# Deformable convolution on one core: a quad's three sampling rounds joined into one visit to the row tiles

## The reference

```python
offset = _offset_conv(x, w_off)            # 3x3, 18 channels: dy, dx of nine taps
py = base_y.astype(x.dtype)[None] + dy
px = base_x.astype(x.dtype)[None] + dx
sampled = _bilinear_gather(x, py, px)      # nine bilinear samples per pixel
return jnp.einsum('bckhw,ock->bohw', sampled, w_conv.reshape(O, C, K * K))
...
x = x + _L0_conv_ref(_ln_c(x), L0_conv_w_off, L0_conv_w_conv)
```

## Time and profile before

| | us |
|---|---|
| median of 3 runs | 3994.7 |
| lowest and highest | 3988.97, 3998.19 |
| span of the profiled execution, first to last instruction | 3990.2 |
| TensorE busy in that span | 3781.9 (95%) |
| VectorE, ScalarE, GpSimd busy | 2579.8, 1794.4, 1553.5 |
| phase A in that span | about 0 to 2100 |

### The profile page before, as it was taken

How to read it: one execution, slowest core, us unless ns; L and a number is a source line. 1 busy time by engine, 2 the same in 40 slices (tenths; PEclk the granted TensorE clock), 3 DMA queues, 4 the chain that set the end, 5 groups by cost and what they waited for, 6 DMA issues and landing times. The chain is left out here.

```text
span 3990.2 us, 88376 instructions
## 1 busy us (share of the span) xinstructions
PE 3781.9 (95%) x31447; PEld 2461.4 (62%) x31447; DVE 2579.8 (65%) x8511; ACT 1794.4 (45%) x4685; POOL 1553.5 (39%) x2661
## 2 busy tenths in 40 slices
PE   6999999999999999999997999999999999997468
PEld 5666666666666666666663566666666666664245
DVE  4444444444444444444426999999999999996633
ACT  4555555555555555555530334344343434344124
POOL 4544545455444544445422333232323233333210
PEclk8999999999999999999997999999999999998755
DMA  6555555555555554555525777777777777885779
GB/s 117 102 97 96 91 93 95 89 101 93 88 97 91 101 92 89 95 91 91 88 47 194 270 276 268 276 269 277 266 278 271 275 271 270 280 300 175 270 292 394
DMA packets 611673, 709.79 MB, mean 178 GB/s; under 512 B 62256, under 2 KB 494256, under 8 KB 594848
## 3 DMA queue, kind: packets, MB, share of 16 engines
q1 hardware_dynamic: 505760, 630.17, 57.1%
q10 hardware_dynamic: 104448, 71.85, 5.8%
q0 software_dynamic: 1024, 2.10, 0.1%
HBM read 521.20 MB, written 181.63 MB: 176 GB/s over the span
## 5 line engine op out<-in xcount | busy, mean ns | idle before, releaser
L366 PE MATMUL a_ob<-a_sr,wcv 128*128 128x512 f32 (+3 forms) x2820 | 1081.6, 518 | 0.8 <-DVE a_xo L496 0.8
L436 ACT COPY a_sr<-a_sb 128x576 f32<-128x576 f32 (+7 forms) x1296 | 621.2, 562 | 903.9 <-PE a_sb L351 895.9
L351 PEld LDWEIGHTS a_sb<-a_tt,a_win 32*128 32x128 f32 x19008 | 655.7, 185 | 264.6 <-issue 247.7
L351 PE MATMUL a_sb<-a_tt,a_win 32*128 32x144 f32 x19008 | 748.6, 300 | 19.2 <-ACT a_sr L436 12.7
L521 POOL TENSOR_TENSOR a_sx<-a_hh 128x576 f32<-128x576 f32 x260 | 377.8, 1453 | 929.9 <-DVE a_hh L473 921.8
L366 PEld LDWEIGHTS a_ob<-a_sr,wcv 128*128 128x128 f32 x2820 | 491.3, 191 | 279.0 <-issue 231.5
L1116 DVE TENSOR_TENSOR b_P<-b_P,b_x 128x1024 f32<-128x1024 f32 x512 | 620.2, 1212 | 1.8 <-DMA b_P<-pd 1.8
L473 DVE TENSOR_SCALAR a_hh<-a_hh 128x576 f32<-128x576 f32 (+1 forms) x128 | 59.5, 465 | 841.0 <-ACT a_hh L415 841.0
L1019 PE MATMUL b_z<-b_P,b_ew 128*128 128x512 f32 x1024 | 463.4, 595 | 0.0
L1022 PE MATMUL b_z<-b_P,b_ew 128*128 128x512 f32 x1024 | 460.3, 592 | 0.0
L1245 POOL TENSOR_TENSOR b_ss<-b_st 128x12 f32<-128x12 f32 (+2 forms) x139 | 30.0, 216 | 1058.1 <-DVE b_pp L1190 963.8
(11 more groups left out here) (186 smaller groups left out, 5302.4 us busy)
## 6 DMA issues: line engine op xcount, KB each, us to landing
b_P<-pd SPq DMA_DIRECT2D x128, 2048.0 KB, 7.6
a_win<-xtp SPq DMA_DIRECT2D x2144, 36.0 KB
a_xin<-in_x SPq DMA_DIRECT2D x128, 256.0 KB, 6.3
xtp<-a_tn ACTq DMA_DIRECT2D x128, 256.0 KB, 2.3
x1d<-a_xo SPq DMA_DIRECT2D x128, 256.0 KB, 5.9
b_x<-x1d SPq DMA_DIRECT2D x128, 256.0 KB, 7.5
x2d<-b_xa SPq DMA_DIRECT2D x128, 256.0 KB, 3.4
pw<-x3d SPq DMA_DIRECT2D x128, 256.0 KB, 6.6
```

The costliest lines, as they stand in the source:

```text
L351: t = e.matmul(d[:, 0:3 * m_, :, NU_ * i:NU_ * i + NU_], win[32 * q:32 * q + 32, half_of(Q, j) % NWH, NWIN // 3 * h + i, :], m, start=(j = ...
L366: t = e.matmul(ob[:, r:r + m, :], k["wcv"][:, 3 * (2 - kr) + kx, :], rows[:, :, t_, :], start=(t_ == 0 and r == 0), stop=(t_ == 8))
L436: a = e.copy(bass.AP(d.tensor, d.offset, [list(d.ap[0]), [1152, ni], [1536, nk], [32, 4], [1, m]]), bass.AP(v.tensor, v.offset, [list(v.ap ...
```

## The change

A quad's three rounds stand together at slot 0 of the step (the small quad's at slot 12). Rounds 0 and 2 write to banks 0 to 3, round 1 to banks 4 to 7. These four are shared with the results of turn (bank 4), conv (5 and 6), shift (6) and out (7). So round 1 waits until the readers of all four are through (normed, mv_ready, y_ready, on_ready, x1_ready), and every full-array matmul waits until round 1's copy is through (bank_free). The second conv of a step, in the shift's bank, waits for on_ready, the offs of the same step. The copy out of the banks is a stage of its own, "evict", at slots 1, 2 and 3: ScalarE copies the quarters 0 and 1, VectorE 2 and 3, and each raises its own semaphore. Round 1's copy is done with two instructions of 432 columns on each engine, the others with three. The full-array work follows from slot 4 on: shift, turn, then out with the two convs between its taps.

```diff
@@ order_a
-        for h in range(3 if len(cs) else 0):
-            samples[t0 + 4 * h] = (quad_of(cs[0]), h)
-            if len(cs) > 4:
-                samples[t0 + 12 + 2 * h] = (quad_of(cs[4]), h)
+        if len(cs):
+            samples[t0] = quad_of(cs[0])
+        if len(cs) > 4:
+            samples[t0 + 12] = quad_of(cs[4])
...
+        if 0 <= Z < NG:
+            put(t0 + 4, "shift", Z)
+            put(t0 + 4, "offs", Z)
         if 0 <= F < NG:
-            put(t0 - 3, "turn", F)
-            put(t0 - 1, "stats", F)
-            put(t0 + 1, "scale", F)
-            put(t0 + 4, "conv", F, 0)
-            put(t0 + 8, "conv", F, 1)
-            put(t0 + 4, "norm", F, 0)
-            put(t0 + 5, "norm", F, 1)
-            put(t0 + 6, "norm_out", F)
-            put(t0 + 6, "y_out", F, 0)
-            put(t0 + 10, "y_out", F, 1)
+            put(t0 + 4, "turn", F)
+            put(t0 + 4, "stats", F)
+            put(t0 + 6, "scale", F)
+            put(t0 + 5, "conv", F, 0)
+            put(t0 + 6, "conv", F, 1)
+            put(t0 + 7, "norm", F, 0)
+            put(t0 + 7, "norm", F, 1)
+            put(t0 + 8, "norm_out", F)
+            put(t0 + 8, "y_out", F, 0)
+            put(t0 + 9, "y_out", F, 1)
         if 0 <= Z < NG:
-            put(t0 - 1, "zsum", Z)
-            put(t0 + 1, "shift", Z)
-            put(t0 + 2, "offs", Z)
-            put(t0 + 3, "offs_out", Z)
-            put(t0 + 4, "reach", Z)
-            put(t0 + 3, "place", Z)
-            put(t0 + 4, "hats", Z)
-            put(t0 + 7, "bend", Z)
-            put(t0 + 9, "clip", Z)
+            put(t0 + 1, "zsum", Z)
+            put(t0 + 5, "offs_out", Z)
+            put(t0 + 5, "place", Z)
+            put(t0 + 5, "hats", Z)
+            put(t0 + 6, "bend", Z)
+            put(t0 + 7, "reach", Z)
+            put(t0 + 7, "clip", Z)
         if 0 <= s - 2 < NG:
-            for t, slot in enumerate((1, 2, 3, 5, 6, 7, 9, 10, 11)):
+            for t, slot in enumerate((4, 5, 6, 7, 8, 9, 10, 11, 11)):
...
-            out.append(("sample", Q, h))
+            out.append(("sample", Q))
+        for h in range(3):
+            if slot - 1 - h in samples:
+                out.append(("evict", samples[slot - 1 - h], h))
@@ phase_a
-    TK = P("a_tk", [128, 4, 128])
-    YO = P("a_yo", [128, 512])
-    YB = [P("a_yb0", [128, 2, 162]), YO[:, 0:324].rearrange("p (r f) -> p r f", r=2)]
-    OF = YO[:, 324:396].rearrange("p (r f) -> p r f", r=4)
-    SB = P("a_sb", [128, 4, 512])
-    OB = P("a_ob", [128, 512])
+    SB = P("a_sb", [128, 8, 512])
+    TK = SB[:, 4, :].rearrange("p (r f) -> p r f", r=4)
+    YB = [SB[:, i, 0:324].rearrange("p (r f) -> p r f", r=2) for i in (5, 6)]
+    OF = SB[:, 6, 324:396].rearrange("p (r f) -> p r f", r=4)
+    OB = SB[:, 7, :]
...
+    def strips(Q, h, q0):
+        n, m_ = quad(Q)
+        b, c = centre(n)
+        R = b * H + c - 1
+        v = SB[:, 4 * (h % 2) + q0, 0:1]
+        if h == 1 and m_ == 4 and c >= 0:
+            for q in (0, 1):
+                d = sr[:, (R - 2) % NSR * 1152 + 12 * h + 32 * (q0 + q):][:, 0:1]
+                yield (bass.AP(d.tensor, d.offset, [list(d.ap[0]), [1152, 4], [1536, 3], [127, 3], [1, 12]]),
+                       bass.AP(v.tensor, v.offset + 512 * q, [list(v.ap[0]), [108, 4], [36, 3], [12, 3], [1, 12]]))
+            return
...
+        for kx in range(3):
+            x = max(0, 12 * h - kx)
+            m = min(31, 12 * h + 11 - kx) + 1 - x
+            for i, ni, kr, nk in parts:
+                d = sr[:, ((R - 2) % NSR + i + kr) * 1152 + kr * 384 + kx * 128 + x + 32 * q0:][:, 0:1]
+                yield (bass.AP(d.tensor, d.offset, [list(d.ap[0]), [1152, ni], [1536, nk], [32, 2], [1, m]]),
+                       bass.AP(v.tensor, v.offset + (9 * i + 3 * kr + kx) * 12 + x + kx - 12 * h,
+                               [list(v.ap[0]), [108, ni], [36, nk], [512, 2], [1, m]]))
@@ tensor
+        def bank_free():
+            w.wait_ge(taken_act, taken)
+            w.wait_ge(taken_dve, taken)
...
             elif o[0] == "conv":
                 _, G, h = o
+                bank_free()
                 w.wait_ge(y_ready, 4 * (G - 1) + 2 * h + 2)
                 if h:
-                    w.wait_ge(on_ready, min(G - 2, NG - 1) + 1)
+                    w.wait_ge(on_ready, shifts)
...
-                w.wait_ge(sr_ready, 3 * Q + h)
-                for i in range(NWIN // 3):
+                for h in range(3):
+                    if h == 1:
+                        w.wait_ge(normed, convs)
+                        w.wait_ge(mv_ready, convs // 2)
+                        w.wait_ge(y_ready, 2 * convs)
+                        w.wait_ge(on_ready, shifts)
+                        w.wait_ge(x1_ready, outs)
+                    else:
+                        w.wait_ge(taken_act, 3 * Q + h // 2)
+                        w.wait_ge(taken_dve, 3 * Q + h // 2)
+                    for i in range(NWIN // 3):
...
+                                d = SB[:, 4 * (h % 2) + q, 0:432].rearrange("p (k t x) -> p k t x", k=12, t=3)
...
+                    t.then_inc(sampled, 1)
+                taken = 3 * Q + 2
@@ scalar
-            elif o[0] == "sample":
+            elif o[0] == "evict":
...
+                for d, v in strips(Q, h, 0):
+                    a = e.copy(d, v)
+                a.then_inc(taken_act, 1)
@@ vector
+            elif o[0] == "evict":
...
+                w.wait_ge(sampled, 3 * Q + h + 1)
+                w.wait_ge(conv_out, (min(R + m_ + 1, b * H + H - 1) - NSR) // 4 + 1)
+                for d, v in strips(Q, h, 2):
+                    a = e.tensor_copy(d, v)
+                a.then_inc(taken_dve, 1)
```

More of the change, by code:

```diff
@@ L230, in order_a @@
         if slot in samples:
-            Q, h = samples[slot]
-            while h == 0 and windows < B * NHALF and (windows < NWH or last_quad(windows - NWH) < Q):
+            Q = samples[slot]
+            while windows < B * NHALF and (windows < NWH or last_quad(windows - NWH) < Q):
                 out.append(("window", windows))
                 windows += 1
-            out.append(("sample", Q, h))
+            out.append(("sample", Q))
+        for h in range(3):
+            if slot - 1 - h in samples:
+                out.append(("evict", samples[slot - 1 - h], h))
         out += at.get(slot, ())
@@ L272, in phase_a @@
         sem(n) for n in ("turned", "convolved", "shifted", "sampled", "conv_out"))
-    normed, y_ready, bent, sr_ready = (sem(n) for n in ("normed", "y_ready", "bent", "sr_ready"))
+    normed, y_ready, bent, taken_act = (sem(n) for n in ("normed", "y_ready", "bent", "taken_act"))
+    taken_dve = sem("taken_dve")
     filled, bn_done, mv_ready, on_ready, reached, clipped, weighed_dve, turned_s, x1_ready = (
@@ L313, in tensor @@
                 _, G, h = o
+                bank_free()
                 w.wait_ge(y_ready, 4 * (G - 1) + 2 * h + 2)
                 if h:
-                    w.wait_ge(on_ready, min(G - 2, NG - 1) + 1)
+                    w.wait_ge(on_ready, shifts)
+                convs += 1
                 for r in range(2):
@@ L323, in tensor @@
                 G = o[1]
+                bank_free()
                 w.wait_ge(z_step, z_count[G])
                 w.wait_ge(on_ready, G)
-                w.wait_ge(y_ready, 4 * min(G + 2, NG))
+                w.wait_ge(y_ready, 2 * convs)
+                shifts += 1
                 for kx in (0, 2):
@@ L354, in tensor @@
-                t.then_inc(sampled, 1)
+                for h in range(3):
+                    if h == 1:
+                        w.wait_ge(normed, convs)
+                        w.wait_ge(mv_ready, convs // 2)
+                        w.wait_ge(y_ready, 2 * convs)
+                        w.wait_ge(on_ready, shifts)
+                        w.wait_ge(x1_ready, outs)
+                    else:
+                        w.wait_ge(taken_act, 3 * Q + h // 2)
+                        w.wait_ge(taken_dve, 3 * Q + h // 2)
+                    for i in range(NWIN // 3):
+                        for j in range(2):
+                            for q in range(4):
+                                u = NU_ * (NWIN // 3 * h + i)
+                                m = tt[32 * q:32 * q + 32, Q % NTP, 1152 * j + u:1152 * j + u + 1]
+                                m = bass.AP(m.tensor, m.offset, [list(m.ap[0]), [96, 3 * m_], [31, 3], [1, NU_]])
+                                d = SB[:, 4 * (h % 2) + q, 0:432].rearrange("p (k t x) -> p k t x", k=12, t=3)
+                                t = e.matmul(d[:, 0:3 * m_, :, NU_ * i:NU_ * i + NU_],
+                                             win[32 * q:32 * q + 32, half_of(Q, j) % NWH, NWIN // 3 * h + i, :], m,
+                                             start=(j == 0), stop=(j == 1))
+                    t.then_inc(sampled, 1)
@@ L455, in vector @@
                 a.then_inc(mv_ready, 1)
+            elif o[0] == "evict":
+                _, Q, h = o
+                n, m_ = quad(Q)
```

(4 more changed lines are left out.)

28 lines of the change are left out of this document (11 added, 17 removed).

## The result

| | before | after |
|---|---|---|
| median, us | 3991.84 (4 runs) | 3886.73 (4 runs) |
| ratio, 95% interval | | 0.9723, 0.9708 to 0.9739 |
| the same pair on another chip | 3997.13 | 3879.56, ratio 0.9704, 0.9691 to 0.9718 |
| span of the profiled execution | 3990.2 | 3883.5 |

The change makes the kernel 2.8% faster. The forecast was 3898 us; 105 us were gained where 97 were forecast. The first view is again the busy time by stretches, with the columns of the earlier trace rows.

What follows compares the result with a forecast made beforehand. TensorE, 99.5% busy in sampling, was taken as the bound. Steps gain 87 + 2, image ends 7, last quad 2, start loses 1: 97 us off 3990.2, plus 4.5 median offset, about 3898 us; range 3878 to 3965.

Steps and rivals of the forecast that it cites:

- the removed visits: TensorE's row tiles, sampling phase: two of three visits per step go, saving 0.81 us a step before stalls.
- Rival (b): Sampling rounds: the gap belongs to each round's first wait and stays, 122 x 0.40 less gained, 3947 us; chance 0.04.
- the 0.19 inside a round: TensorE's sampling round: takes 1.81 us where twelve groups of matmuls need 1.62; priced as part of each row-tile visit.
- The convs: TensorE's conv matmuls: 0.65 us after a round, 0.55 expected behind out, so 2 x 0.10 us saved a step.
- The waits inside the visit: PSUM copies between joined rounds: round 0's end by 3.08 us, round 2 could start at 3.33, slack 0.2 us.
- rival (d): VectorE's strided PSUM copies cost more than contiguous ones; at twice the price about 4125 us; chance of slower 0.08.
- threshold of 1.82 us: VectorE's copy visit: at this length, 1.6 times the price taken, late round 2 and second conv eat the 0.81 us.
- The chains behind the visit: After the copies: offs before the second conv, slack 0.27 us; y_out before the next step's round 1, slack 0.85 us.
- The stall of 0.10 us a step: TensorE's steps: allowance for three waits with small slacks, bounds 0 and 0.35 us, leaving 0.71 us gain a step.
- three slacks: Round 2, the second conv and the next step's round 1: slacks of 0.2, 0.27 and 0.85 us.
- The start: First 50 us, clock 0.83: turn now stands behind shift, 1 us lost, bounds -3 to +4.
- Image ends and tail: Small quad's rounds at three image ends: 2.3 us gained each, three times 7; the last small quad 2.

Runs made afterwards that it cites:

- the tiny matmuls: Changed kernel plus tiny four-column full-array matmuls ahead of rounds 1 and 2: one per gap 4018.69 us (ratio 1.0047), two per gap 4083.47 us (run once).
- the other execution: The changed kernel itself, unmodified, run again on another chip beside the start variants: 3879.56 us, ratio 0.9704 to the kernel before.

## Why the prediction was right

**What bounds the kernel, and the removed visits.** Right. The step is 14.89 us; it was to be 14.93 without stalls. In the parts: the visit 5.03 (5.05), out 7.82 (7.84), convs 0.55 each (0.55), shift and turn as before. Rival (b) said that the 0.19 inside a round stays with every round. It does not: rounds 1 and 2 of a visit have waits of their own, already met, and take 1.62. What is true in it is that 0.10 of the 0.19 comes back behind every wait that is not met, and behind a tiny matmul on one row tile.

**The convs.** Right in its size, loose in its reason. I put the 0.10 down to the convs that stand behind a round. It belongs to whatever stands behind a visit: the tiny matmuls show 0.09 there. It went away because two visits did.

**The waits inside the visit.** All six times came within 0.05 us: VectorE's copies started at 1.94, 3.55 and 5.14 us of the visit (predicted 1.92, 3.54, 5.16) and were 1.11, 1.12 and 0.96 long (1.12, 1.13, 0.98). ScalarE's first three took 0.94 where 1.1 was taken (1213.14 us in its timeline). VectorE copies the strided runs at the price of the contiguous row: 432 columns take 603 ns, 0.15 + 432 x 1.04 is 600. So the condition of rival (d) was not met. The run in which VectorE copies everything shows that its mechanism works and that its threshold of 1.82 us is near the truth. The overlap of 0.08 us at each joint held as well: 0.457 + 0.422 + 0.397 is 1.28, and the three take 1.11.

**The chains behind the visit.** offs ended 7.69 us into the step (8.02), the second conv began at 8.23 (8.29): 0.5 us slack, not 0.27. y_out ended at 16.1 (15.8), since scale took 2.26 us and y_out 1.86 where 1.91 and 1.60 were taken; slack 0.5, not 0.85. Neither ran out.

**The stall of 0.10 us a step.** A term that was mis-sized: it is nearly nil. With three slacks of 0.2 us or more, the sum said zero and I added a tenth for jitter. From the fourth visit on, the image ends apart, 110 of 118 distances between visits lie within 0.1 us of 14.89, and eight are 0.1 to 1.1 us longer, 3.3 us together: 0.03 us a step. The tenth was 12 us, more than the whole miss of the forecast.

**The start.** Mis-sized, and its cause missed: 1 us, bounds -3 to +4, against 9.9 in the profile and some 5 in the other execution. I priced turn behind shift and left out that round 1 now waits for y_out at the start too, with no out work yet to fill the time: 2.80 and 4.34 us of idle time ahead of it in visits 1 and 2. The chain y_out, round 1, copies, offs, norm, y_out takes 15.7 us there (64.09 to 79.78), where the same chain by my prices is some 14.3. I put the rest down to round 1 at the lower clock (its copy starts 3.0 us behind it, at 67.10, instead of 1.8): I had seen the clock row and didn't carry it into the chain.

**Image ends and tail.** The three passages from the small quad to the next, 7.98, 7.62 and 8.52 us, are 5.19 each: 8.6 shorter, of which 1.3 is the turn that moved elsewhere. That leaves 7.2, and 7 were forecast. From the last visit on 5.1 were gained where I had 2.

**How the terms add up.** The steps gained more than forecast (0.84 us each where 0.71 was taken, some 16 us over the phase) and the last visits and the tail 4; the start lost 9 more and the later phases 1. That the total came within 11 us is in part luck, because the steps and the start missed in opposite ways. Either miss alone would have left the time inside the range.

## What to carry to other kernels

Price a visit to the row tiles by its three places (on entry behind a wide matmul, in the first group, ahead of the next work) and count the visits; here it was 0.4 us each, 0.8 of 15.7 us a step. The first group's part comes back after every wait that is not met, so joined rounds must not wait. Joining the visits takes away the work that hid the copies out of PSUM, so it only wins with a second set of banks, and the copies' length then decides: write the times of one step down from the visit's first matmul, and where the slack is several times the scatter of the steps, add nothing for jitter. Work out the start of the pipeline on its own, at the clock that it runs at, with every wait that the change adds and without the work that hides it later.

## What the runs showed of the hardware

- A sampling round that starts after an unmet wait pays twice. From the end of the copy to its first matmul it took 0.05 us with one semaphore to wait for (either engine copying everything) and 0.15 us with two (all rounds in banks 0 to 3). Its first group of four took 0.10 us more than the others.
- The first group takes 0.24 us instead of 0.13 behind full-array work, behind an unmet wait and behind one tiny matmul on a row tile alike.
- A single matmul of four columns on one of four row tiles cost 0.21 us a gap, about as much as one on the full array without the way out of the row tiles and back (0.22).
- VectorE copied PSUM to SBUF in runs of 12 columns at 0.15 us + 1.04 ns a column (603 ns for 432), the price of 512 contiguous columns in the last phase.
- The granted clock over the first 50 us was 0.74 and 0.90 in two executions of the same program on two chips; visit 0 began 7 us apart.
